# Row sums on TensorE by 32-column f32 matmuls on the raw chunk, and rows 0 to 2 of the first phase taken whole

## The reference

```python
adj_hat = adj + eye(N)
d = 1 / sqrt(sum(adj_hat, axis=1))
out = (adj_hat * d[:, None] * d[None, :]) @ (x @ W) + b
x = layernorm(x + relu(out))
o = relu(x @ W1 + adj @ (x @ W1) + x @ Wself)
x = layernorm(x + pair_norm(o))
```

## Time and profile before

| | us |
|---|---|
| median of 3 runs | 1891.78 (1887.06 to 1892.68) |
| the profiled execution's own time | 1891.55 |
| its span, first to last instruction | 1889.8 |
| TensorE matmul busy | 1752.6 (93%) |
| VectorE busy | 1488.8 (79%) |
| ScalarE busy | 1205.6 (64%) |

### The profile page before, as it was taken

How to read it: one execution, slowest core, us unless ns; L and a number is a source line. 1 busy time by engine, 2 the same in 40 slices (tenths; PEclk the granted TensorE clock), 3 DMA queues, 4 the chain that set the end, 5 groups by cost and what they waited for, 6 DMA issues and landing times.

```text
span 1889.8 us, 20584 instructions
## 1 busy us (share of the span) xinstructions
PE 1752.6 (93%) x7682; PEld 1418.1 (75%) x7682; DVE 1488.8 (79%) x1985; ACT 1205.6 (64%) x1640; POOL 21.3 (1%) x42
## 2 busy tenths in 40 slices
PE   2879998987999999989999999999989999999993
PEld 1657886865887888767788888888868888877872
DVE  4889788767878789986777575575589999999997
ACT  4576685784757556654554554455468888888875
POOL 0000000000000000100000000000000000000001
PEclk7899999998999999999999999999999999999995
DMA  9999999899898686954544445555589999999943
GB/s 398 421 421 421 417 400 422 337 392 394 348 402 345 234 356 244 358 197 148 174 163 189 167 175 197 182 178 189 191 304 385 385 388 386 386 379 366 386 193 89
DMA packets 87459, 572.03 MB, mean 303 GB/s; under 512 B 8960, under 2 KB 17152, under 8 KB 19264
## 3 DMA queue, kind: packets, MB, share of 16 engines
q1 hardware_dynamic: 84928, 562.07, 75.8%
q0 software_dynamic: 2432, 8.65, 1.4%
HBM read 566.49 MB, written 4.19 MB: 302 GB/s over the span
## 4 chain that ended last, share of the span: by engine, by line
PE 74%; DVE 14%; DMA 6%; ACT 4%; issue 2%; SPq 0%; ACTq 0%; DVEq 0%
PE acc L1043 18%; PE acc L1045 18%; PE acc L1049 18%; DMA raw<-in_adjT 4%; PE pC L1025 4%; PE pD L1025 4%; DVE raw_low L726 4%; DMA s<-in_adjN 2%; ACT hi L558 2%; DVE o_low L726 1%; DVE s L732 1%; DVE zr_low L726 1%; DVE ux L805 1%; PE pA L1043 1%; PE pB L1045 1%
## 5 line engine op out<-in xcount | busy, mean ns | idle before, releaser
L1043 PE MATMUL acc<-hi,rhi 128*128 128x512 f32 x1792 | 726.3, 405 | 76.3 <-DVE raw_low L726 25.0
L726 DVE TENSOR_TENSOR raw_low<-raw,hi 128x1024 fp32r<-128x1024 f32 x576 | 684.3, 1220 | 84.4 <-ACT hi L558 79.8
L558 ACT ACTIVATE hi<-raw 128x1024 fp32r<-128x1024 f32 x576 | 593.7, 1055 | 195.3 <-DMA raw<-in_adjT 68.3
L1049 PE MATMUL acc<-hi,rlo 128*128 128x512 f32 x1792 | 559.9, 394 | 0.0
L1045 PE MATMUL acc<-raw_low,rhi 128*128 128x512 f32 x1348 | 530.7, 394 | 0.0
L1043 PEld LDWEIGHTS acc<-hi,rhi 128*128 128x128 f32 x1792 | 341.7, 191 | 173.4 <-DVE raw_low L726 35.0
L1049 PEld LDWEIGHTS acc<-hi,rlo 128*128 128x128 f32 x1792 | 341.2, 190 | 73.7
L1045 PEld LDWEIGHTS acc<-raw_low,rhi 128*128 128x128 f32 x1348 | 256.2, 190 | 54.9 <-issue 3.6
L726 DVE TENSOR_TENSOR zr_low<-zr,hi 128x1024 fp32r<-128x1024 f32 x148 | 177.6, 1221 | 30.4 <-ACT hi L558 27.9
L558 ACT ACTIVATE hi<-zr 128x1024 fp32r<-128x1024 f32 x148 | 155.2, 1059 | 58.4 <-PE pD L1025 24.0
L725 DVE TENSOR_TENSOR rlo<-zr,rhi 128x256 fp32r<-128x256 f32 x123 | 52.0, 423 | 177.5 <-ACT hi L558 177.5
(11 more groups left out here) (187 smaller groups left out, 1813.9 us busy)
## 6 DMA issues: line engine op xcount, KB each, us to landing
raw<-in_adjT SPq DMA_DIRECT2D x288, 1024.0 KB, 5.1
zr<-in_adjT SPq DMA_DIRECT2D x74, 1024.0 KB, 5.4
raw<-in_adjN SPq DMA_DIRECT2D x67, 1024.0 KB, 13.8
o<-in_adjT SPq DMA_DIRECT2D x32, 1024.0 KB, 11.0
s<-in_adjT SPq DMA_DIRECT2D x26, 1024.0 KB, 16.6
zr<-in_adjN SPq DMA_DIRECT2D x23, 1024.0 KB, 11.7
s<-in_adjN SPq DMA_DIRECT2D x22, 1024.0 KB, 12.4
s<-in_xT POOLq DMA_DIRECT2D x8, 512.0 KB, 7.0
```

The costliest lines, as they stand in the source:

```text
L558: S.activation(hi[n % DEEP][:, :], slice_of(chunk, j), ACT.Copy).then_inc(hi_ready, 1)
L726: V.tensor_sub(low_of(chunk, j), slice_of(chunk, j), hi[n % DEEP][:, :].bitcast(f32)).then_inc(slice_split, 1)
L1043: T.matmul(banks[h][:, :], a, hi[n % DEEP][:, part], start=opens, stop=False, skip_group_check=True)
L1049: last = T.matmul(banks[h][:, :], b, hi[n % DEEP][:, part], start=False, stop=end, skip_group_check=True)
```

## The change

`add_sums` no longer uses `hi` and `low`. It runs once per chunk, ahead of the chunk's products, and waits for the chunk's landing only. Four f32 matmuls read the raw chunk, one for each slice and half, each with 32 stationary columns (`QUARTER`) and with an output of 32 partitions of its own: pC 0 to 31, pD 32 to 63, pC 64 to 95, pD 96 to 127. `turn_degree` adds the four strips, since its moving operand `quarters` has ones at k, 32+k, 64+k and 96+k.

The raw bytes of a summed chunk now have to stay until its sums are taken, so `low` can't be written over them. The `low` of summed chunks goes in turn into the bytes of `raw4` and `raw5`, which leave the ring until the last summed chunk; the ring of the first phase is two buffers shorter.

`PARTS` is gone: a stage is a whole row, with the products of the whole row before it. `take_degree` is folded into `degree`. The choice of which `sum` chunks VectorE takes is written differently, and stays one in four after row 0 and one in two in row 0.

```diff
-    PARTS = {0: ((0,), (1,), (2, 3)), 1: ((0, 1), (2, 3)), 2: ((0, 1), (2, 3))}
-    units = []
-    for k in range(NB):
-        units += [(k, qs) for qs in PARTS.get(k, ((0, 1, 2, 3),))]
...
+    for k in range(NB):
         sums = []
         for c in range(k + 1, NB):
...
+            for q in range(Q):
+                sums.append(Chunk("sum", k, c, q, act=(q % 2 == 0 if k == 0 else q != 3), stage=k))
...
+            if chunk.summed:
+                chunk.low = summed % LOWS
+                summed += JB
+                last_summed = slices
...
-    free_buffers = deque([(f"raw{r}", ()) for r in range(6)] + [(b, ()) for b in BORROWED])
+    FOR_LOWS = ("raw4", "raw5")
+    free_buffers = deque([(f"raw{r}", ()) for r in range(4)] + [(b, ()) for b in BORROWED])
...
+        if phase == 2 and not own:
+            own = True
+            free_buffers.extend((b, ("multiplied", last_summed)) for b in FOR_LOWS)
...
-            def add_sums(chunk, n):
-
-                pe.wait_ge(sums_read, closed[0])
-                to = pick[:, NB - 1 - chunk.row:NB - 1 - chunk.row + P]
-                for h in range(H):
-                    for mov in (hi[n % DEEP][:, :], low_of(chunk, n - chunk.base)):
-                        last = T.matmul(sums[h][:, :], to, mov[:, h * HALF:(h + 1) * HALF],
-                                        start=False, stop=False, skip_group_check=True)
-                return last
+            def add_sums(chunk):
+
+
+                pe.wait_ge(*landed(chunk))
+                pe.wait_ge(sums_read, closed[0])
+                to = pick[:, NB - 1 - chunk.row:NB - 1 - chunk.row + QUARTER].bitcast(f32)
+                for t in range(JB * H):
+                    j, h = t // H, t % H
+                    T.matmul(sums[h][t * QUARTER:(t + 1) * QUARTER, :], to,
+                             slice_of(chunk, j)[:, h * HALF:(h + 1) * HALF], start=False, stop=False,
+                             skip_group_check=True)
 
             def multiply(chunk):
                 v = visits[chunk.visit]
+                if chunk.summed:
+                    add_sums(chunk)
                 for j in range(JB):
...
-                    if chunk.summed:
-                        last = add_sums(chunk, n)
                     last.then_inc(slice_multiplied, 1)
```

More of the change, by code:

```diff
@@ L19 @@
     summed: bool = False
+    low: int = -1
     stage: int = -1
@@ L105, in graph_kernel @@
     beside = defaultdict(list)
-    for u, (k, qs) in enumerate(units):
+    for k in range(NB):
         sums = []
         for c in range(k + 1, NB):
[L109 to L112, removed]
+            for q in range(Q):
+                sums.append(Chunk("sum", k, c, q, act=(q % 2 == 0 if k == 0 else q != 3), stage=k))
+        kept = [Chunk("keep", k, k, q, stage=k) for q in range(Q)]
+        if k == 0:
@@ L113, in graph_kernel @@
             chunks += kept + sums
             continue
-        by, of = units[u - 1]
         first = len(products)
[L118 to L122, removed]
+        multiply_block(products, k - 1, k - 1, (L0,), new_visit(k - 1, (L0,), 1, first=(k == 1)),
+                       cached=True, stage=k)
@@ L123, in graph_kernel @@
+        for i in range(k, NB):
+            multiply_block(products, i, k - 1, (L0,), new_visit(i, (L0,), 1, first=(k == 1)),
+                           summed=True, stage=k)
         for i, c in EXTRA.get(k, ()):
-            multiply_block(products, i, c, (L0,), new_visit(i, (L0,), 1), stage=u)
+            multiply_block(products, i, c, (L0,), new_visit(i, (L0,), 1), stage=k)
         for n in range(first, len(products)):
             products[n].tail = n - (len(products) - TAIL)
-        assert not kept or 2 * len(of) + TAIL <= len(products) - first
@@ L130, in graph_kernel @@
[L130 to L138, removed]
+        at = max(2 * Q, min(3 * Q, len(sums)))
+        if k >= NB - 2:
+            sums += [None] * (at - len(sums))
@@ L139, in graph_kernel @@
+        sums[at:at] = kept
+        room = [1.0] * Q + [0.5 if k < NB - 2 else 1.0] * Q + [1.0] * (len(products) - TAIL - first - Q)
         share, put = len(sums) / sum(room), 0
@@ L143, in graph_kernel @@
             upto = round(share * sum(room[:n + 1]))
-            beside[first - lead + n] += [c for c in sums[put:upto] if c]
+            beside[first - Q + n] += [c for c in sums[put:upto] if c]
             put = max(put, upto)
@@ L186, in graph_kernel @@
     after_row0 = next(c for c in chunks if c.stage == 1)
-    slices = act_sums = dve_sums = 0
+    LOWS = 2 * JB
+    slices = act_sums = dve_sums = summed = 0
     for chunk in chunks:
@@ L218, in graph_kernel @@
         while phase < 3 and free_buffers[0][0] in BORROWED and (
-                phase == 2 or units[chunk.stage][0] > BORROWED[free_buffers[0][0]]):
+                phase == 2 or chunk.stage > BORROWED[free_buffers[0][0]]):
             free_buffers.popleft()
@@ L239, in graph_kernel @@
     kept_end = {(c.row, c.q): c.base + JB for c in chunks if c.cached}
-    act_sums_of = [sum(1 for c in chunks if c.kind == "sum" and c.act and c.stage <= u) for u in range(NU)]
-    dve_sums_of = [sum(1 for c in chunks if c.kind == "sum" and not c.act and c.stage <= u) for u in range(NU)]
+    act_sums_of = [sum(1 for c in chunks if c.kind == "sum" and c.act and c.stage <= k) for k in range(NB)]
     free = {0: (), 1: (), 2: (("x1", NB * 2),), 3: (("s1", NB * 2), ("self", NB * 2))}
@@ L545, in split_hi @@
                     if l == L0:
[L546 removed]
+                        act.wait_ge(z_ready, chunk.col + 1)
                     else:
@@ L639, in _ @@
                         sum_rows(chunk)
-                    if chunk.stage == 0 and chunk.col == 3 and chunk.q == 0:
+                    if chunk.stage == 0 and chunk.col == 1 and chunk.q == 2:
                         read_sums(0)
@@ L649, in _ @@
                 after_rows(n)
-                if chunk.tail == 2 and opens_row(chunk.stage):
-                    read_sums(units[chunk.stage][0])
+                if chunk.stage > 0 and chunk.tail == 2:
+                    read_sums(chunk.stage)
                 if chunk.stage > 0 and chunk.tail == 5:
@@ L946, in _ @@
                 after_rows(n)
-                if chunk.tail == 4 and opens_row(chunk.stage):
-                    take_degree(units[chunk.stage][0])
                 if chunk.stage > 0 and chunk.tail == 4:
```

91 lines of the change are left out of this document (43 added, 48 removed).

## The result

| | before | changed |
|---|---|---|
| median, us (4 runs each) | 1890.65 | 1866.83 (1865.1 to 1868.05) |
| the profiled execution's own time | 1891.55 | 1867.01 |
| its span | 1889.8 | 1865.2 |

The ratio is 0.9875 with a 95% interval of [0.9863, 0.9887]: 24 us faster. The forecast was 1956; the side is rival A's, the size about half of A's. All times here are of fast executions; of experiment 11 one more took 5883.6 us and is left out.

What follows compares the result with a forecast made beforehand. First phase: DMA and TensorE nearly in balance, DMA full early, TensorE busy later. Row sums +77, start +52, gaps and low clock -65 give +64 on 1891.55, said as 1956; range 1835 to 2010, the forecast's own 1910 to 2000.

Steps and rivals of the forecast that it cites:

- rival A: The strips' sums run fully side by side: S 1.20, phase end 718 to 733, time near 1844; chance 0.28.
- S: What a chunk's row sums cost TensorE in us; forecast 2.50 with the width change, bounds 2.14 and 2.84, old sums 1.81.
- a third value: Eight recorded sum matmuls in strict program order need five places of 0.427, so 2.14 us before the width change.
- The width change: TensorE going from full width to strips and back around a chunk's sums: 0.36 us taken, nearest two tails.
- Term 1: Row sums on TensorE: 112 chunks x (2.50 - 1.81) = +77 us.
- Term 2: Start: whole row 0 must land before z, so the first product comes at 98 instead of 46.1, +52 us.
- Term 3: TensorE's gaps (46.7) and low clock (up to 28) in the first phase go, 10 kept: -65 us.
- Term 4: Ring two buffers shorter and raw bytes held longer: nothing as long as TensorE is the later one.
- Terms 5 and 6: Low parts in raw4 and raw5, VectorE's and ScalarE's work, and the products after 774: nothing.
- the break-even: The cost of a chunk's sums at which the change gains nothing: 1.93 us.
- Rival B: No sum matmuls run side by side: S 3.77, +206 us, 2098; chance 0.16.
- signs: Sums to product 2.5 us (rival A 1.2, Rival B 3.8); row 1's DMA share about 0.86, or 1.0 for rival A.

Runs made afterwards that it cites:

- experiment 11: Changed kernel with the strip sums of two chunks taken in one go, the even chunk's buffer held half a chunk longer; 1884.01 us, ratio 0.9968.
- experiment 3: Changed kernel with all four f32 sum matmuls of a chunk in one strip; 2101.74 us, one execution.
- experiment 4: Changed kernel with two strips used in pairs (0, 0, 1, 1) for a chunk's four sum matmuls; 1915.18 us, one execution.
- experiment 14: Changed kernel with each chunk's sums taken one chunk ahead, raw4 and raw5 out of the ring holding nothing; 1883.99 us, ratio 0.9965.
- 13: Changed kernel with each chunk's sums taken one chunk ahead, low in place, six own buffers in the ring; 1865.74 us, ratio 0.9871.
- experiment 2: Kernel before with the new strip sums and the ring two buffers shorter, PARTS kept; 1872.13 us, ratio 0.9911.
- experiments 5 to 7: Changed kernel with sums between a chunk's two slices (1868.66 us), with kept chunks' sums on TensorE instead of VectorE's adds (1864.63), and with both (1867.72).
- experiment 10: Whole rows and old sums, with the changed kernel's ring, two buffers shorter; 1897.96 us, ratio 1.0042.
- experiment 9: Changed kernel without the column sums of the 112 summed chunks, with six own buffers in the ring; 1839.32 us, ratio 0.9732.
- experiment 1: Kernel before with rows 0 to 2 whole, old sums and six own buffers kept; 1891.41 us, ratio 1.001.

## Why the prediction was wrong

**The step that failed** is the choice of S: "a third value that follows if matmuls start strictly in program order", and "I take this one" (2.14, with the width change 2.50). Measured is 1.23. The evidence given for it, that all matmuls in the rows start in order, came from matmuls that all use the full width, so none of them could have gone past another; and the experiments 3 and 4 show the order bends as soon as there are strips. The width change was sized well: 0.36 forecast, 0.38 measured. The Trainium skill, "TensorE: Matmul & The Clock Gate", Part 3, says that matmuls start and end in strict program order; four first halves within 0.02 us, and the fifth of eight matmuls starting ahead of three waiting ones, don't agree with it across strips, and the measurement decides. The figures for tiles side by side on the same page of the Trainium skill, from which the prediction worked out 1.03 for S, were far nearer than its rule of order.

**Term 1** would be, with the measured S, 112 x (1.20 - 1.81) = -68 instead of +77, and busy time fell by 67.9. **Term 2**, the start: 98 forecast, 98.8 measured, with some luck. Load 35 and ScalarE's three sum chunks ahead of `rhi` came as described (the last chunk's passes begin at 92.51), but the terms given, 92.6 + 2 x 1.06 + 1.0 + 1.0, add up to 96.7 and not to 98. What the prediction left out is VectorE's own sum chunk of row 1, which stands ahead of its first split:

```profile
95.00 2.29 DVE L730 TENSOR_REDUCE s<-s 128x2 f32<-128x2048 f32 x1 [2.90 <-DMA s<-in_adjN]
97.20 0.42 DVE L723 TENSOR_TENSOR rlo<-zr,rhi 128x256 fp32r<-128x256 f32 x1
97.54 2.35 DVE L724 TENSOR_TENSOR o_low<-o,hi 128x1024 fp32r<-128x1024 f32 x2
```

**Term 3**, gaps and low clock that go, -65: with the old sums it was 35.8 + 18.9 = 54.7. The gaps were right to a microsecond (10 kept, 10.9 measured); the low clock's 28 was called an upper bound, and 18.9 of it was to be had. In the changed kernel the condition of the term ("with S = 2.50 a stage's TensorE work is longer than its loads") is gone, and not-busy time is 53.2. **Term 4**, the ring, nothing: wrong by 6 to 8 us with the old sums, 18 at the new S (experiment 14 against 13), and 2 to 3 without sums. I take from these three that it costs most where loads and TensorE need about the same time, but only three points stand behind that. **Terms 5 and 6**: VectorE's and ScalarE's busy times are as forecast or lower, and what follows the phase takes 1116.8 to 1121.4 us in the kernels with whole rows and 1117.7 in experiment 2, against 1115.8 before: 1 to 6 us more, for which I have no cause.

**The sum itself holds where TensorE is the later one.** By 1891.6 + 112 x (S - 1.93), S = 3.67 gives 2086 and S = 2.01 gives 1901; measured 2102 and 1915. With S = 1.81 it gives 1878; measured 1891. They are off by 15, 15 and 13, nearly a constant: the low clock's 9 and the 2 to 3 behind the phase make up 11 to 12 of it. So the break-even was at 1.81 with the long ring, and somewhat below with the short one, and not at 1.93; a true S of 2.50 would have come out near 1970 (an estimate from 1915 + 112 x 0.49). Under 1.81 the line bends, since the loads take over: for S = 1.20 it gives 1810, and 1867 was measured.

**Rival A** had the mechanism and the S (1.20) right and was 13 to 28 us too early with its end, 718 to 733 for 746.4. Two sizes were off. It gave z of row 3 eight us behind the last landing at 444 and only its own stages' work from there; but behind `close_sums` at 443.9 stand seven more summed chunks of stage 3, with row 3's `first_product` among them at 464.4, and stage 4's products begin at 478.1: 7 x 3.94 = 28 us where 8 was allowed, +20. (Row 3's small matmuls, 5 us more, and three chunks of stage 7 that lie behind the phase's end, 8 less, nearly cancel.) And it had no gaps in stages 4 to 7; the windows show 87.1 - 80.0, 71.7 - 64.6, 65.9 - 63.7 and 77.8 - 74.5, in all 19.7. Its 706 plus 20 plus 20 is 746. The 12 to 27 that it put on the ring are in those gaps and not beside them; how they divide between the ring, VectorE's adds (4.67 us a chunk in place of 3.94 at some) and the waits behind `close_sums` (7.6 us in the whole phase) was not separated, and experiments 5 to 7 show that the last two can be taken away with next to no gain.

**Where the gain went.** Of 68 us of TensorE's work, 25.6 came out as time. The other 42 are gaps, which grew from 10.9 to 53.2. Of the 53.2, 33.5 lie in stages 1 to 3, where the loads run at their full rate; the 19.7 in stages 4 to 7 are those of the paragraph above. The shorter ring has a part in both: without it (against experiment 10) 73.4 us of work gave 33.5. Leaving out all sums (experiment 9) shows the limit of the loads most plainly: 155 us less busy than experiment 1, and 53 less time. (155 and not 203, since the products that are left run at a granted clock of 0.92 in place of 1.00.) **Rival B** is experiment 3: 2098 forecast for S = 3.77, 2102 measured; the closeness is partly luck, as S was 0.10 lower and the rest of the sum 15 us short. What the prediction named as signs did tell: 1.0 us to the product (A's 1.2 less the way into the strips, ahead of the first sum), DMA share of row 1's stage still at 1.01 (A).

## What to carry over

Evidence on order or overlap from instructions that compete for the same part of an engine says nothing on instructions that don't; where one such step decides the sign, leave its two ends their full weight. Once two resources are level, work taken from one is worth only what lies above the other: here 0.38 us for each us of TensorE's, and 0.46 with the ring held the same. And give every buffer that leaves a ring a price: two of them cost 18 us here at the new S (experiments 13 and 14), where leaving all the sums out of the changed kernel gives 25.

## What was unexpected of the hardware

- Matmuls of 32 stationary columns in different strips start within 0.02 us of each other, also across waiting ones: in program order A, A', B, B' (A' waiting for A's strip) B starts with A (A at 613.55 and B in the same group in experiment 4; 605.84 and 605.85 in the changed kernel).
- An f32 matmul costs about 0.43 us for each of its two halves whether its stationary operand has 32 or 128 columns (606.65 - 605.79 = 0.86 for both halves in experiment 3, 0.85 before); the weight load takes 106 to 107 ns for 32 columns (below) and 188 for 128.
- Going from full width to strips and back costs 0.38 us in all (1.23 - 0.85).

L1013 by source in the changed kernel (duration ns min/median/max, first and last start):

```profile
L1013 PEld LDWEIGHTS pC<-raw,pick x240: 106/107/155, 117.3 to 721.2; 128*32 128x32 f32 x120
L1013 PE MATMUL pC<-raw,pick x240: 589/593/709, 117.3 to 721.6; 128*32 128x512 f32 x120
```
